# One transfer in place of eight for the negated row maxima of an attention step

## The chip, the cores and the metric

The kernel runs on one core of one Trainium2 chip. The metric is the device time of one execution in microseconds (us); the median of three runs of the kernel before is 1428.19 us (1427.73 to 1429.76). The engines are called as in the profile: PE is TensorE (matmuls), PEld its weight loads, DVE is VectorE, ACT is ScalarE, POOL is GpSimd, SP is SyncE, which here issues all DMAs.

## The reference

Two layers over x of shape (8, 512, 512), both conditioned on an embedding. Layer 0 is a linear attention (softmax of q over the features of a head, of k over the tokens). Layer 1 is the one that the change touches: 16 heads of 32, full attention over 512 tokens, with the softmax over the keys.

```
q = (xn @ q_w + q_b).reshape(Bx, Tx, H, -1)
k = (xn @ k_w + k_b).reshape(Bx, Tx, H, -1)
att = jnp.einsum('bnhl,bmhl->bnmh', q, k)
att = att + (1.0 - mask) * -1000000.0
att = jax.nn.softmax(att, axis=2)
v = ((xn @ v_w + v_b) * src_mask[:, :, None]).reshape(Bx, Tx, H, -1)
y = jnp.einsum('bnmh,bmhl->bnhl', att, v).reshape(Bx, Tx, Dx)
h = layer_norm(y, sb_norm_w, sb_norm_b) * (1.0 + scale) + shift
h = jax.nn.silu(h) @ out_w + out_b
return x + h
```

Everything is float32; products are made as three matmuls of high and low parts.

## The kernel before, in words

Layer 0 takes about the first 530 us. Layer 1 is cut into 32 steps: step n = 4b + g is the group g of four heads (j = 0..3) of batch b. Each step needs these items:

- `qk`: the q and k projections of the step, 12 matmuls each (lines 527 to 529), split into high and low parts by ACT (line 885) and DVE (line 1162, `sg_q`, `sg_k`), written to `stack_scratch` (lines 1491, 1492) and read back in stacked form into `Qs[n % 2]` and `Ks[n % 2]` (item `stack`, line 1504, 768 KB each).
- `S`: 16 matmuls (line 686) give the scores with queries on the partitions. DVE takes the negated maximum of each row from PSUM (line 1171, tile `cT`, which `nx` is a view of). ACT takes exp with this as bias (line 894) for the sum of the row only.
- `nxt`: the 16 columns of negated maxima (4 heads x 4 query tiles) are split into a high and a low part by three small DVE reductions (lines 1183, 1185, 1188, tile `nxs`), turned by a DVE transpose (line 1192, `nxT`), and written by SP into rows 98 and 99 of `Qs` (line 1524).
- `a`: 16 matmuls (line 694) give the transposed scores, keys on the partitions. They contract over 100 rows, and rows 98 and 99 subtract the maximum. ACT takes exp into `Pb` (line 904).
- `pv`: 128 small matmuls (line 712) of the step before, `tl` the transpose of their result (line 1199).

So the first `a` matmul of a step cannot start before the maxima of all 16 `S` tiles of that step are in `Qs`. This is called the handoff below. In the transpose before, the column t * 32 + s of `nxs` belongs to query tile t, and DVE turns blocks of 32x32; the maxima of 32 queries are then in four partitions of one block, and each of the two parts of each of four blocks goes by a DMA of its own, 16 pieces of 128 bytes. The eight DMAs of a step are issued back to back by SP.

Between the steps' own items lie the other products of layer 1: `v` (values of the next batch), `o` (output projection of the batch before), `tx` and `ty` (transposes, line 522). The order of all items is made by `the_order`: `weave` merges tracks of items by positions that the table `PLAN` gives, one entry for each g of 0 to 3, and names with a leading z for the last batch. Every engine works off its part of this one order, in order. PSUM has eight banks; the eighth is kept for `pv` in layer 1, seven are given in turn to the rest by `the_banks`, so a matmul may also wait for the reader of the bank's last content.

The wait at the handoff stands in `a` (on `nxq0` or `nxq1`), with a count of 128 for each use of a buffer. On SP the order is also strict: a DMA that stands behind the eight issues starts after them, among them the `stack` loads.

Of the kernel before, what the change touches and what calls it, by code (L numbers as in the profile page):

```python
# [20 lines left out]
RM, RX, RE = 96, 98, 100  # L21
# [20 lines left out]


PLAN = {
    "0k": ((0.157, 0.58), (0.489, 0.551)),
    "0v": ((0.811, 1.12), (0.011, 0.573)),
    "0q": ((0.678, 1.186), (0.109, 0.533), (1.018, 1.051)),
    "0o": ((0.808, 1.15), (0.725, 0.935), (0.176, 0.444)),
    "att": ((0.053, 0.062, 0.082, 0.233, 0.461), (0.01, 0.088, 0.245, 0.401, 0.741), (0.093, 0.109, 0.262, 0.692, 0.887), (0.349, 0.494, 0.559, 0.616, 0.645)),
    "pv": ((0.043,), (0,), (0,), (0.041,)),  # L50
    "tl": (None, (0.467, 1.131), (0.214, 0.217), (0.603, 0.7)),
    "tlx": ((0.277, 0.483), None, None, None),
    "ty": ((0, 0.854, 1.112), (0, 0.98, 1.049), (0, 1.11, 1.155), (0, 1.13, 1.169), (1, 0.038, 0.177)),
    "S": ((0.422, 0.55, 0.742, 0.811, 0.898), (0.396, 0.525, 0.936, 1.048, 1.099), (0.477, 0.9, 1.006, 1.108, 1.192), (0.066, 0.069, 0.727, 0.814, 0.999)),
    "nxt": ((0.923, 1.15), (1.106, 1.131), (1.173, 1.2), (1.183, 1.186)),
    "q": ((0.103, 0.141, 0.49), (0, 0, 0.086), (0.018, 0.115, 0.135), (0.049, 0.185, 0.238)),
    "k": ((0.527, 0.575, 0.782), (0.051, 0.192, 0.44), (0.243, 0.573, 0.583), (0.163, 0.432, 0.506)),
    "stack": ((1.2, 1.2), (0.696, 0.806), (0.756, 0.999), (0.602, 0.932)),
# [8 lines left out]
    "zatt": ((0.389, 0.877, 1.078, 1.121, 1.2), (0.088, 0.154, 0.355, 0.428, 0.525), (0.127, 0.319, 0.671, 1.024, 1.029), (0.181, 0.534, 0.601, 1.155, 1.2)),  # L67
    "zpv": ((0.273,), (0.111,), (0,), (0,)),
    "ztl": (None, (0.056, 1.025), (0.855, 1.141), (0.296, 0.516)),
    "ztlx": ((0.31, 0.95), None, None, None),  # L70
    "zty": ((0, 1.189, 1.2), (0, 1.199, 1.2), (1, 0, 0.319), (2, 1.157, 1.168), (3, 0.116, 0.835)),
    "zS": ((0.106, 0.211, 0.313, 0.395, 0.658), (0.55, 0.609, 0.778, 0.878, 1.016), (0.06, 0.243, 0.412, 0.43, 0.472), (0.163, 0.184, 0.449, 0.715, 0.933)),
    "znxt": ((1.063, 1.119), (1.183, 1.183), (1.14, 1.174), (0.381, 0.999)),
    "zq": ((0.487, 0.551, 0.824), (0.092, 0.2, 0.294), (0.518, 0.638, 1.2), (0.016, 0.077, 0.568)),
    "zk": ((0.834, 1.067, 1.139), (0.422, 0.431, 0.432), (0.295, 0.422, 0.904), (0.258, 0.961, 1.163)),
    "zstack": ((1.164, 1.192), (0.768, 1.042), (0.787, 1.2), (0.878, 1.019)),
    "tle": (None, None, None, (0.468, 0.924)),
    "zz": ((0.485, 0.776), (0.556, 0.808), (1.128, 1.2), (1.131, 1.2)),
    "lr": ((0.321, 0.774), None, None, None),
    "1v": ((0.569, 0.995), (0.143, 0.675), (0.449, 0.607)),  # L80
}


# [204 lines left out]
def cond_two_layers(nc, A, out):  # L288
# [4 lines left out]
    with ctx:  # L293
        def sb(name, shape, dt=F32, c=ctx):
            return c.enter_context(nc.sbuf_tensor(name, shape, dt))
# [38 lines left out]

        dn = sb("dn", [128, 2, NT, H1])
        nx = cT[:].rearrange("p a b -> p (a b)").rearrange("p (n j t s) -> p n j t s", n=2, j=4, s=2)
        nxs = sb("nxs", [128, NT, 32], FR)
        nxT = sb("nxT", [128, NT * 32])
        identr = sb("identr", [128, 128], FR)
        ident = identr[:].bitcast(F32)  # L340

# [31 lines left out]
        Qs, Ks = [None, None], [None, None]  # L373
# [139 lines left out]
        def _(e):  # L513
            def take(key):
                p = bank_before[key]
                if p is not None:
                    e.wait_ge(*done(p))
                return ps[bank_of[key]]
# [170 lines left out]
            def a(i, n, m, j):  # L689
                par = n % 2  # L690
                bank = take(("a", n, m, j))
                if m == 0 and j == 0:
                    e.wait_ge(s[f"nxq{par}"], 128 * (n // 2 + 1))
                e.matmul(bank[:], Ks[par][0:RE, j, m * 128:(m + 1) * 128], Qs[par][0:RE, j, :],  # L694
                         start=True, stop=True).then_inc(s["ST"], 1)

# [216 lines left out]
        def _(e):  # L913
# [317 lines left out]
            def tlx(i, b):  # L1231
# [7 lines left out]
                if i in (1, 3):  # L1239
# [112 lines left out]
        def _(e):  # L1352
# [232 lines left out]
```

## Time and profile before

| | before |
|---|---|
| median of 3 runs | 1428.19 us |
| profiled execution, its own time | 1433.99 us |
| span in the profile | 1432.2 us |
| mean granted TensorE clock | 0.955 of full |
| PE busy | 1322.4 us, 92% |
| DVE busy | 1023.1 us, 71% |
| ACT busy | 1001.6 us, 70% |
| POOL busy | 344.9 us, 24% |

Busy times are over the whole span. In layer 0 ACT does little, so its share in layer 1 is higher than 70%; the table by stretches in the rows below shows this. Idle time of an engine is named by what ended it. A chain of waits goes back from the last instruction to what released it at each step. In the table by stretches the five busy times are those of PE, PEld, DVE, ACT and POOL, in this order, and the granted clock (PEclk) is a share of full speed. The time between the span and the execution's own time, 1.8 us, lies around the kernel's instructions.

### The profile page before, as it was taken

The numbers are of one execution on the slowest core, as the hardware profiler recorded it, in microseconds if no ns is written. First come the engines' busy times: TensorE is split into PE (matmuls) and PEld (weight loads), VectorE is DVE, ScalarE is ACT, GpSimd is POOL, SyncE is SP. The second block draws the span as 40 slices with busy tenths as digits, with TensorE's granted clock in tenths as the row PEclk, the third lists the DMA queues.
The fourth block names the chain that finished last, engine by engine and source line by source line (L and its number), as shares of the span: only waits on it lengthen the run. The fifth ranks groups of instructions, "written<-read, shape, count | busy, mean of one in ns | idle before, by whom it ended". The sixth has DMA issues, their size and how long they took to land.

```text
span 1432.2 us, 25785 instructions
## 1 busy us (share of the span) xinstructions
PE 1322.4 (92%) x9592; PEld 1060.3 (74%) x9592; DVE 1023.1 (71%) x2025; ACT 1001.6 (70%) x2259; POOL 344.9 (24%) x367
## 2 busy tenths in 40 slices
PE   8899999999999988898998998998998898998898
PEld 5788888888888766576776776776776686676556
DVE  5887878888789874576766766756765865766555
ACT  4445445445455557897897887887897897898874
POOL 0323344234432520102402402402400500500203
PEclk9999999999999997998998998999999999999969
DMA  9011131111322455743544544544544454454412
GB/s 333 30 38 59 38 96 37 60 59 38 96 73 83 136 149 179 210 140 126 156 142 148 142 153 140 154 134 148 155 121 149 147 150 149 134 164 118 141 39 89
DMA packets 88029, 173.79 MB, mean 121 GB/s; under 512 B 12360, under 2 KB 12360, under 8 KB 87904
## 3 DMA queue, kind: packets, MB, share of 16 engines
q1 hardware_dynamic: 87904, 172.14, 39.3%
q8 instruction: 76, 1.25, 0.4%
q14 instruction: 49, 0.40, 0.1%
HBM read 104.45 MB, written 67.14 MB: 120 GB/s over the span
## 4 chain that ended last, share of the span: by engine, by line
PE 58%; DVE 17%; SPq 10%; DMA 7%; ACT 3%; issue 3%; POOL 1%; DVEq 0%; ACTq 0%; POOLq 0%
PE ps L527 12%; PE ps L529 12%; PE ps L528 12%; PE ps L694 9%; DVE cT L1171 8%; SPq L1524 8%; PE ps L686 5%; PE ps L522 3%; DMA Ks<-stack_scratch 3%; DMA Qs<-nxT 2%; PE ps L712 2%; ACT ps L894 1%; PE ps L636 1%; PE ps L615 1%; DMA mask_scratch<-vhl 1%
## 5 line engine op out<-in xcount | busy, mean ns | idle before, releaser
L1171 DVE TENSOR_REDUCE cT<-ps 128x1 f32<-128x512 f32 x512 | 323.3, 681 | 146.8 <-PE ps L686 146.0
L894 ACT ACTIVATE ps<-ps,cT 128x512 f32<-128x512 f32 x512 | 342.7, 683 | 35.8 <-DVE cT L1171 34.9
L904 ACT ACTIVATE Pb<-ps 128x512 f32<-128x512 f32 x512 | 269.1, 626 | 106.5 <-PE ps L694 103.6
L694 PE MATMUL ps<-Qs,Ks 100*128 100x512 f32 x512 | 182.3, 444 | 60.1 <-DMA Qs<-nxT 54.3
L686 PE MATMUL ps<-Ks,Qs 98*128 98x512 f32 x512 | 186.8, 428 | 21.9 <-ACT ps L894 10.1
L694 PEld LDWEIGHTS ps<-Qs,Ks 100*128 100x128 f32 x512 | 105.0, 210 | 101.7 <-issue 60.9
L686 PEld LDWEIGHTS ps<-Ks,Qs 98*128 98x128 f32 x512 | 98.3, 193 | 70.2 <-ACT ps L894 33.4
L1342 POOL TENSOR_TENSOR yb<-yb,cU 128x512 f32<-128x512 f32 x14 | 20.1, 1452 | 483.5 <-DVE cU L1215 483.5
L894 ACT ACTIVATION_READ_ACCUMULATOR ps<-ps,cT 128x1 f32 x512 | 116.1, 227 | 0.0
L527 PE MATMUL ps<-xTh,Wh_k 128*128 128x512 f32 x256 | 108.1, 422 | 6.8 <-DVE xTl L1022 3.7
L1266 POOL TENSOR_TENSOR rs<-ve,mhalf 128x4 f32<-128x4 f32 x32 | 32.6, 1019 | 334.0 <-DVE ve L990 218.0
L527 PE MATMUL ps<-Wh_o,sTh 128*128 128x512 f32 x256 | 103.6, 404 | 2.6 <-DVE sTl L1148 2.5
L527 PE MATMUL ps<-Wh_v,xTh 128*128 128x512 f32 x256 | 103.0, 402 | 0.0
L529 PE MATMUL ps<-xTh,Wl_k 128*128 128x512 f32 x256 | 102.1, 399 | 0.0
L528 PE MATMUL ps<-xTl,Wh_k 128*128 128x512 f32 x256 | 102.0, 399 | 0.0
L528 PE MATMUL ps<-Wl_o,sTh 128*128 128x512 f32 x256 | 100.7, 393 | 0.0
L528 PE MATMUL ps<-Wl_v,xTh 128*128 128x512 f32 x256 | 100.5, 393 | 0.0
L529 PE MATMUL ps<-Wh_v,xTl 128*128 128x512 f32 x256 | 100.5, 393 | 0.0
L529 PE MATMUL ps<-Wh_o,sTl 128*128 128x512 f32 x256 | 100.5, 393 | 0.0
L1308 POOL TENSOR_TENSOR wr<-wr,boB 128x512 f32<-128x512 f32 x64 | 82.9, 1313 | 9.8 <-DMA wr<-x_scratch 5.2
L1162 DVE SCALAR_TENSOR_TENSOR sg_q<-ps,cols,sg_q 128x512 fp32r<-128x512 f32 x32 | 23.9, 748 | 58.2 <-ACT sg_q L885 58.2
L1022 DVE TENSOR_TENSOR xTl<-ps,xTh 128x512 fp32r<-128x512 f32 x64 | 43.5, 689 | 29.8 <-ACT ps L774 29.7
(169 smaller groups left out, 2946.3 us busy)
## 6 DMA issues: line engine op xcount, KB each, us to landing
Qs<-stack_scratch SPq DMA_DIRECT2D x32, 768.0 KB
Ks<-stack_scratch SPq DMA_DIRECT2D x32, 768.0 KB
stack_scratch<-sg_q SPq DMA_DIRECT2D x32, 512.0 KB, 2.7
stack_scratch<-sg_k SPq DMA_DIRECT2D x32, 512.0 KB, 2.6
wr<-in_x SPq DMA_DIRECT2D x32, 256.0 KB, 4.9
x_scratch<-wr SPq DMA_DIRECT2D x32, 256.0 KB, 2.5
stack_scratch<-sg_q SPq DMA_DIRECT2D x32, 256.0 KB, 2.9
stack_scratch<-sg_k SPq DMA_DIRECT2D x32, 256.0 KB, 2.9
```

Of the source, the lines that this page charges most:

```text
L522: r = e.transpose(bank[:, t * 128:(t + 1) * 128], src, ident)
L527: e.matmul(bank[:], lh(k), rh(k), start=(k == 0), stop=False)
L528: e.matmul(bank[:], lh(k), rl(k), start=False, stop=False)
L529: return e.matmul(bank[:], ll(k), rh(k), start=False, stop=(k == NC - 1))
L686: e.matmul(bank[:], Qs[par][0:RX, j, t * 128:(t + 1) * 128], Ks[par][0:RX, j, :], start=True, stop=True).then_inc(s["S"], 1)
L694: e.matmul(bank[:], Ks[par][0:RE, j, m * 128:(m + 1) * 128], Qs[par][0:RE, j, :], start=True, stop=True).then_inc(s["ST"], 1)
L894: e.activation(bank[:], bank[:], ACT.Exp, bias=nx[:, n % 2, j, t, 0:1], accum_out=dn[:, b % 2, t, 4 * g + j:4 * g + j + 1]).then_inc(s["S_ ...
L904: e.activation(Pb[m][:, j, :], ps[bank_of["a", n, m, j]][:], ACT.Exp).then_inc(s["P"], 1)
L1022: e.tensor_tensor(xTl[:, c, :], ps[bank_of["tx", x, c]][:], xTh[:, c, :].bitcast(F32), ALU.subtract).then_inc(s["xT_lo"], 1)
L1171: e.tensor_reduce(nx[:, n % 2, j, t, 0:1], ps[bank_of["S", n, j, t]][:], AX.X, ALU.max, negate=True).then_inc(s["S_max"], 1)
L1308: e.tensor_tensor(wr[t][:], wr[t][:], boB[:], ALU.add).then_inc(s["xb"], 1)
L1524: e.dma_start(row.bitcast(F32), src).then_inc(s[f"nxq{par}"], 16)
```

## The change

Four things change in the code. The tile `nxs` becomes 32 columns wide (16 high, 16 low parts), column order head, query tile. The one transpose of 128x128 becomes four of 32x32, one for each group of 32 partitions, put side by side into `nxT` of 32 rows and 128 columns. One DMA moves these 32 rows of 512 bytes into rows 98 and 99 of `Qs`. The semaphore's count goes from 128 to 16 for each use. And the table `PLAN` has new numbers throughout.

```diff
-        nxs = sb("nxs", [128, NT, 32], FR)
-        nxT = sb("nxT", [128, NT * 32])
+        nxs = sb("nxs", [128, 32], FR)
+        nxT = sb("nxT", [32, 128])
...
                 if m == 0 and j == 0:
-                    e.wait_ge(s[f"nxq{par}"], 128 * (n // 2 + 1))
+                    e.wait_ge(s[f"nxq{par}"], 16 * (n // 2 + 1))
...
-                    m = nx[:, n % 2].rearrange("p j t s -> p t j s")
-                    hi = nxs[:, :, 0:4]
+                    m = nx[:, n % 2].rearrange("p j t s -> p (j t) s")
+                    hi, lo = nxs[:, 0:16], nxs[:, 16:32]
...
-                    e.transpose(nxT[:], nxs[:].rearrange("p t c -> p (t c)").bitcast(F32)).then_inc(s["nx_tr"], 1)
+                    for u in range(4):
+                        r = e.transpose(nxT[:, 32 * u:32 * u + 32], nxs[32 * u:32 * u + 32, :].bitcast(F32))
+                    r.then_inc(s["nx_tr"], 1)
...
-                    for u in range(4):
-                        for r in range(2):
-                            row = Qs[par][RX + r:RX + r + 1, :, :].rearrange("p j (t n) -> p j t n", t=NT)[:, :, :, 32 * u:32 * u + 32]
-                            src = nxT[32 * u + 4 * r:32 * u + 4 * r + 4, :].rearrange("j (t n) -> j t n", t=NT)
-                            e.dma_start(row.bitcast(F32), src).then_inc(s[f"nxq{par}"], 16)
+                    e.dma_start(Qs[par][RX:RE, :, :].bitcast(F32).rearrange("s j (t n) -> s (j t) n", t=NT),
+                                nxT[:]).then_inc(s[f"nxq{par}"], 16)
...
 PLAN = {
-    "nxt": ((0.923, 1.15), (1.106, 1.131), (1.173, 1.2), (1.183, 1.186)),
+    "nxt": ((0.889, 1.004), (1.116, 1.173), (1.195, 1.195), (1.074, 1.163)),
...
```

What stands on DVE ahead of the handoff to step 16 (the first step of a batch), before. `cT` are the row maxima, `bvB` the bias of the values (item `v`), `nxs` and `nxT` the parts of the maxima and their transpose; ps0 to ps7 are the banks.

```order
L1171 TENSOR_REDUCE cT<-ps4 128x1 [waits s_S]
L1171 TENSOR_REDUCE cT<-ps3 128x1 [waits s_S]
L1171 TENSOR_REDUCE cT<-ps2 128x1 [waits s_S]
L1070 TENSOR_TENSOR ps6<-ps6,bvB 128x512 [waits s_v_mm]
L1070 TENSOR_TENSOR ps1<-ps1,bvB 128x512 [waits s_v_mm]
L1183 TENSOR_REDUCE nxs<-cT 128x4x4 [waits s_S_max,s_nx_tr]
L1185 TENSOR_REDUCE cT<-nxs 128x4x4 [waits s_nx_hi]
L1188 TENSOR_REDUCE nxs<-cT 128x4x4 [waits s_nx_neg]
L1192 STREAM_TRANSPOSE nxT<-nxs 128x128 [waits s_nx_lo,s_nxq1]
```

And the same place on DVE now:

```order
L1171 TENSOR_REDUCE cT<-ps5 128x1 [waits s_S]
L1070 TENSOR_TENSOR ps0<-ps0,bvB 128x512 [waits s_v_mm]
L1171 TENSOR_REDUCE cT<-ps1 128x1 [waits s_S]
L1171 TENSOR_REDUCE cT<-ps6 128x1 [waits s_S]
L1183 TENSOR_REDUCE nxs<-cT 128x16 [waits s_S_max,s_nx_tr]
L1185 TENSOR_REDUCE cT<-nxs 128x16 [waits s_nx_hi]
L1188 TENSOR_REDUCE nxs<-cT 128x16 [waits s_nx_neg]
L1193 STREAM_TRANSPOSE nxT<-nxs 32x32 [waits s_nx_lo,s_nxq1]
L1193 STREAM_TRANSPOSE nxT<-nxs 32x32 x3
L1070 TENSOR_TENSOR ps4<-ps4,bvB 128x512 [waits s_v_mm]
```

The two additions of the values' bias stood between the last maximum and the splitting; now one stands ahead of the last two maxima and the other behind the transposes.

What SP issues around the handoff to step 17 (the second step of a batch), before. `sg_q` and `sg_k` are the projections on their way out, `Qs<-stack_scratch` and `Ks<-stack_scratch` the loads for the step after.

```order
L1491 DMA stack_scratch<-sg_q 128x1024 [waits s_q1_lo,s_stack0]
L1492 DMA stack_scratch<-sg_q 128x512
L1491 DMA stack_scratch<-sg_k 128x1024 [waits s_k1_lo,s_stack0]
L1492 DMA stack_scratch<-sg_k 128x512
L1524 DMA Qs1<-nxT 1x16x32 [waits s_nx_tr,s_ST]
L1524 DMA Qs1<-nxT 1x16x32 x7
L1504 DMA Qs0<-stack_scratch 96x4x512 [waits s_stq0,s_ST]
L1504 DMA Ks0<-stack_scratch 96x4x512 [waits s_stk0]
```

And now, at the same place on SP:

```order
L1493 DMA stack_scratch<-sg_q 128x1024 [waits s_q1_lo,s_stack0]
L1494 DMA stack_scratch<-sg_q 128x512
L1493 DMA stack_scratch<-sg_k 128x1024 [waits s_k1_lo,s_stack0]
L1494 DMA stack_scratch<-sg_k 128x512
L1522 DMA Qs1<-nxT 2x16x128 [waits s_nx_tr,s_ST]
L1506 DMA Qs0<-stack_scratch 96x4x512 [waits s_stq0,s_ST]
L1506 DMA Ks0<-stack_scratch 96x4x512 [waits s_stk0]
```

Nothing changed places here; the loads stand behind one issue in place of eight.

On PE the work between the last `S` matmul of a step and its first `a` matmul is nearly as before: three parts of `v` and `pv` at g = 0, three of `ty`, `pv` and three of `qk` at g = 1, `tx`, `pv` and two or three others at g = 2; at g = 3 four parts of `qk` and five `S` of the next step in place of six and six. In the first steps of the last batch there is more of it than before.

## Rows read from the trace of the kernel before

**Rows 1.** Table by stretches: us, then busy us (and count), PEclk, DMA share, GB/s.
```profile
0.00:530.00 530.00, 515.24 (x2752) 430.74 (x2753) 437.45 (x945) 266.27 (x528) 186.42 (x205) 0.99 0.28 89
...
860.00:970.00 110.00, 99.44 (x865) 79.55 (x864) 74.53 (x136) 93.15 (x221) 21.58 (x22) 0.95 0.49 145
```

**Rows 2.** The chain that ended last, by line, from the page.
```profile
PE ps L527 12%; PE ps L529 12%; PE ps L528 12%; PE ps L694 9%; DVE cT L1171 8%; SPq L1524 8%; PE ps L686 5%; PE ps L522 3%; DMA Ks<-stack_scratch 3%; DMA Qs<-nxT 2%; PE ps L712 2%; ACT ps L894 1%; PE ps L636 1%; PE ps L615 1%; DMA mask_scratch<-vhl 1%
```

**Rows 3.** Waits over the span: us in total, times, longest.
```profile
ACT Pb L904 <- PE ps L694: 103.6, 51, 7.9
...
PE ps L694 <- DMA Qs<-nxT: 54.3, 23, 5.0
...
PEld ps L686 <- ACT ps L894: 33.4, 70, 1.3
...
PE ps L686 <- DMA Ks<-stack_scratch: 8.4, 5, 2.1
```

**Rows 4.** Timeline, handoff to step 16: start, us, what [idle before <- releaser].
```profile
974.80 2.47 DVE L1171 TENSOR_REDUCE cT<-ps 128x1 f32<-128x512 f32 x4
...
978.08 3.70 PE L712 MATMUL ps<-Pb,vf 128*32 128x128 f32 x128
978.19 0.70 DVE L1070 TENSOR_TENSOR ps<-ps,bvB 128x512 f32<-128x512 f32 x1 [0.30 <-PE ps L529]
...
978.79 0.17 DVE L1183 TENSOR_REDUCE nxs<-cT 128x16 fp32r<-128x16 f32 x1
...
979.90 5.32 SPq L1524 DMA_DIRECT2D Qs<-nxT  x8
...
986.42 4.18 PE L694 MATMUL ps<-Qs,Ks 100*128 100x512 f32 x9 [4.64 <-DMA Qs<-nxT]
...
987.28 4.51 ACT L904 ACTIVATE Pb<-ps 128x512 f32<-128x512 f32 x9 [7.52 <-PE ps L694]
```

**Rows 5.** Timeline of PE: other handoffs, to steps 0, 18 and the last one.
```profile
536.93 4.18 PE L694 MATMUL ps<-Qs,Ks 100*128 100x512 f32 x9 [4.92 <-DMA Qs<-nxT]
...
1046.91 0.93 PE L694 MATMUL ps<-Qs,Ks 100*128 100x512 f32 x3 [1.18 <-DMA Qs<-nxT]
...
1373.73 0.47 PE L694 MATMUL ps<-Qs,Ks 100*128 100x512 f32 x1 [3.17 <-DMA Qs<-nxT]
```

**Rows 6.** Timeline of SP and PE at step 17, and the loads behind the issues.
```profile
1014.79 0.48 SPq L1504 DMA_DIRECT2D Ks<-stack_scratch  x1
...
1015.46 0.70 PE L694 MATMUL ps<-Qs,Ks 100*128 100x512 f32 x2
...
1023.98 0.77 PE L686 MATMUL ps<-Ks,Qs 98*128 98x512 f32 x1 [2.03 <-DMA Ks<-stack_scratch]
```

**Rows 7.** SP's issue times of line 1524, ns min/median/max.
```profile
L1524 SPq DMA_DIRECT2D Qs<-nxT x256: 623/623/768, 530.3 to 1390.3; - x128
```

**Rows 8.** Timeline of SP ahead of the handoff to step 19.
```profile
1058.20 0.32 SPq L1504 DMA_DIRECT2D Qs<-stack_scratch  x1
...
1068.44 5.32 SPq L1524 DMA_DIRECT2D Qs<-nxT  x8
```

**Rows 9.** Small DVE groups by shape: busy us, mean ns, idle before.
```profile
L1192 DVE STREAM_TRANSPOSE nxT<-nxs 128x128 f32<-128x128 f32 x32 | 10.0, 311 | 3.7 <-DVE nxs L1188 0.5
...
L965 DVE TENSOR_SCALAR mod<-ps,cols 128x8 f32<-128x8 f32 x8 | 1.2, 218 | 0.4 <-PE ps L550 0.4
...
L1044 DVE DVE_READ_ACCUMULATOR2_ANT kmx<- 128x1 f32 x32 | 2.6, 83 | 0.0
```

**Rows 10.** Table by stretches behind the handoff to step 16, columns as in Rows 1.
```profile
987.00:990.00 3.00, 3.00 (x9) 2.35 (x8) 2.37 (x7) 2.72 (x6) 0.00 (x0) 0.50 0.89 329
990.00:994.00 4.00, 4.00 (x13) 3.17 (x12) 0.00 (x0) 2.39 (x5) 0.00 (x0) 0.61 0.71 264
```

**Rows 11.** Timeline of ACT in the same stretch.
```profile
992.34 0.60 ACT L904 ACTIVATE Pb<-ps 128x512 f32<-128x512 f32 x1 [0.55 <-PE ps L694]
...
994.41 3.05 ACT L904 ACTIVATE Pb<-ps 128x512 f32<-128x512 f32 x6 [1.47 <-PE ps L694]
```

More of the change, by code:

```diff
@@ L44 @@
 PLAN = {
[L45 to L52, printed above, removed]
@@ L53 @@
-    "ty": ((0, 0.854, 1.112), (0, 0.98, 1.049), (0, 1.11, 1.155), (0, 1.13, 1.169), (1, 0.038, 0.177)),
-    "S": ((0.422, 0.55, 0.742, 0.811, 0.898), (0.396, 0.525, 0.936, 1.048, 1.099), (0.477, 0.9, 1.006, 1.108, 1.192), (0.066, 0.069, 0.727, 0.814, 0.999)),
-    "nxt": ((0.923, 1.15), (1.106, 1.131), (1.173, 1.2), (1.183, 1.186)),
-    "q": ((0.103, 0.141, 0.49), (0, 0, 0.086), (0.018, 0.115, 0.135), (0.049, 0.185, 0.238)),
-    "k": ((0.527, 0.575, 0.782), (0.051, 0.192, 0.44), (0.243, 0.573, 0.583), (0.163, 0.432, 0.506)),
@@ L58 @@
-    "stack": ((1.2, 1.2), (0.696, 0.806), (0.756, 0.999), (0.602, 0.932)),
[8 rows of a table removed]
[L67 to L79, printed above, removed]
@@ L80 @@
-    "1v": ((0.569, 0.995), (0.143, 0.675), (0.449, 0.607)),
+    "0k": ((0.063, 0.764), (0.503, 1.092)),
+    "0v": ((0.889, 1.145), (0.111, 0.562)),
+    "0q": ((0.659, 1.176), (0, 0.263), (1.065, 1.134)),
+    "0o": ((1.083, 1.166), (0.409, 1.001), (0.43, 0.514)),
+    "att": ((0.067, 0.22, 0.238, 0.274, 0.346), (0.092, 0.203, 0.203, 0.28, 0.842), (0.057, 0.091, 0.523, 0.582, 0.776), (0.194, 0.516, 0.534, 0.578, 0.583)),
+    "pv": ((0.02,), (0.012,), (0,), (0.031,)),
+    "tl": (None, (0.227, 0.827), (0.359, 0.894), (0.218, 0.556)),
@@ new lines @@
+    "tlx": ((0.202, 0.373), None, None, None),
+    "ty": ((0, 0.844, 0.993), (0, 0.971, 0.974), (0, 0.995, 1.056), (0, 1.098, 1.131), (1, 0.102, 0.57)),
+    "S": ((0.385, 0.541, 0.753, 0.843, 0.878), (0.428, 0.527, 0.815, 1.009, 1.08), (0.629, 0.928, 1.047, 1.186, 1.196), (0.047, 0.057, 0.759, 0.789, 0.966)),
+    "nxt": ((0.889, 1.004), (1.116, 1.173), (1.195, 1.195), (1.074, 1.163)),
+    "q": ((0.221, 0.255, 0.708), (0.046, 0.08, 0.125), (0.012, 0.092, 0.131), (0.041, 0.152, 0.248)),
+    "k": ((0.447, 0.553, 0.802), (0.2, 0.239, 0.462), (0.271, 0.409, 0.548), (0.358, 0.415, 0.53)),
@@ new lines @@
+    "stack": ((1.121, 1.174), (0.614, 0.861), (0.792, 1.063), (1.018, 1.032)),
[8 rows of a table added]
+    "zatt": ((0.516, 1.051, 1.154, 1.164, 1.2), (0.081, 0.676, 0.704, 0.834, 0.883), (0.629, 0.705, 0.878, 1.065, 1.076), (0.188, 0.286, 0.473, 0.724, 0.85)),
+    "zpv": ((0.186,), (0,), (0.158,), (0.332,)),
+    "ztl": (None, (0.768, 1.2), (0.525, 0.906), (0.525, 1.2)),
+    "ztlx": ((0.196, 1.045), None, None, None),
+    "zty": ((0, 1.199, 1.199), (0, 1.2, 1.2), (1, 0, 0.163), (1, 0.098, 0.64), (2, 0.352, 1.039)),
@@ new lines @@
+    "zS": ((0, 0.053, 0.168, 0.53, 0.58), (0.792, 0.945, 0.96, 1.031, 1.148), (0.084, 0.109, 0.136, 0.157, 0.367), (0.077, 0.089, 0.375, 0.382, 0.67)),
+    "znxt": ((0.958, 1.04), (1.12, 1.146), (0.405, 0.595), (0.228, 0.936)),
+    "zq": ((0.448, 0.642, 0.987), (0, 0.011, 0.271), (0.096, 0.394, 1.085), (0.249, 0.701, 1.13)),
+    "zk": ((0.627, 0.725, 0.955), (0.287, 0.345, 0.475), (0.093, 1.119, 1.2), (0.843, 0.898, 0.97)),
+    "zstack": ((1.129, 1.2), (0.821, 0.825), (0.61, 0.701), (0.131, 0.723)),
@@ L81 @@
+    "tle": (None, None, None, (1.021, 1.191)),
+    "zz": ((0.637, 0.772), (0.717, 0.973), (0.875, 1.2), (1.088, 1.2)),
+    "lr": ((0.093, 0.131), None, None, None),
+    "1v": ((0.21, 0.861), (0.354, 0.971), (0.113, 0.944)),
 }
@@ L1182, in nxt @@
                     e.wait_ge(s["S_max"], 16 * n + 16)
-                    e.tensor_reduce(hi, m[:, :, :, 0:1], AX.X, ALU.max).then_inc(s["nx_hi"], 1)
+                    e.tensor_reduce(hi, m[:, :, 0:1], AX.X, ALU.max).then_inc(s["nx_hi"], 1)
                     e.wait_ge(s["nx_hi"], n + 1)
-                    e.tensor_reduce(m[:, :, :, 1], hi.bitcast(F32).unsqueeze(3), AX.X, ALU.max, negate=True).then_inc(s["nx_neg"], 1)
+                    e.tensor_reduce(m[:, :, 1], hi.bitcast(F32).unsqueeze(2), AX.X, ALU.max, negate=True).then_inc(s["nx_neg"], 1)
                     e.wait_ge(s["nx_neg"], n + 1)
                     with nc.allow_low_precision(reason="the sum of a number and its negated high part is exact"):
-                        e.tensor_reduce(nxs[:, :, 4:8], m, AX.X, ALU.add).then_inc(s["nx_lo"], 1)
+                        e.tensor_reduce(lo, m, AX.X, ALU.add).then_inc(s["nx_lo"], 1)
                     if n:
-                        e.wait_ge(s[f"nxq{(n - 1) % 2}"], 128 * ((n - 1) // 2 + 1))
+                        e.wait_ge(s[f"nxq{(n - 1) % 2}"], 16 * ((n - 1) // 2 + 1))
                     e.wait_ge(s["nx_lo"], n + 1)
-                    e.transpose(nxT[:], nxs[:].rearrange("p t c -> p (t c)").bitcast(F32)).then_inc(s["nx_tr"], 1)
+                    for u in range(4):
+                        r = e.transpose(nxT[:, 32 * u:32 * u + 32], nxs[32 * u:32 * u + 32, :].bitcast(F32))
+                    r.then_inc(s["nx_tr"], 1)
             def tl(i, n):
```

16 rows, old and new, of the table PLAN are left out of this document.

## The prediction

> **What bounds the kernel now.** The page's shares name PE as the busiest engine. The table by stretches [rows 1] says where it isn't busy: layer 0 (530 us) has PE at 97% (515.24 / 530) and a clock of 0.99, so nothing is to be had there, and the change touches nothing there but the order. In layer 1 a batch of four steps takes about 110 us; PE is busy 99.4 of them, idle 10.6, with a mean clock of 0.95. A mean of 0.95 between the levels 2.4 and 1.2 GHz means 10% of the time at the lower one, 11 us, of which half, 5.5 us, are lost. ACT is busy 93.2 of 110, DVE 74.5. So layer 1 is bound by PE with ACT close behind.
>
> The chain [rows 2] shows what breaks PE's work: 8% of it (115 us) is SP issuing the maxima's DMAs, 2% their flight. The chain would promise over 100 us, but it charges the issues even where PE had other work meanwhile. The list of waits is the better measure [rows 3]: PE waited 54.3 us in 23 handoffs, the longest 5.0. ACT waited 103.6 us for the `a` matmuls, because it has nothing between its last `S` and the first `a`.
>
> The timeline of one handoff [rows 4] gives the parts. The last maximum ends at 974.80 + 2.47 = 977.27. Two bias additions follow, the second late by 0.30, so the splitting starts at 978.79, and 1.5 us have gone. Reductions, transpose (0.31, rows 9) and gaps take the 1.11 until 979.90, the eight issues last to 985.22, and 1.2 us later, at 986.42, PE starts. It had been free since 978.08 + 3.70 = 981.78. Of this kind (g = 0, waits of 4.6 to 5.0, the first at 536.93 [rows 5]) there are seven. At g = 2 the wait is about 1.2, in the last batch up to 3.2 [rows 5]. At g = 1 none is shown: PE has its own work until 1015.46 [rows 6].
>
> **Issues, eight to one.** An issue takes 0.623 [rows 7], the row of eight 5.32 [rows 4]. One issue of the new shape isn't in the trace: from below a stack load's 0.32 [rows 8], from above the longest of this line, 0.77 [rows 7]. I take 0.62, since it goes between the same tiles. That is 4.7 us off each handoff (bounds 4.55 to 5.0).
>
> **Transposes, one to four.** One of 128x128 takes 0.311. The trace has none of 32x32. From below, the shortest DVE instruction is 0.083, so four would be 0.33; from above, four at 0.311 are 1.24. The nearest row is the run of small operations without waits between them, 0.218 each [rows 9]: 0.87, so +0.56 a handoff (bounds 0.0 to 0.9). On DVE alone that is 18 us over 32 steps; DVE is busy 74.5 of 110, and its waits on PE hide it. It counts only as a later handoff.
>
> **Flight.** 32 pieces of 512 bytes in place of 128 of 128 bytes, 16 KB both times. From issue end to PE it was 1.2 [rows 4]. I keep 1.2, bounds 0.8 to 3.
>
> Four pieces of 512 bytes carry what sixteen of 128 did, which speaks for less; what could speak against it is the spread over DMA engines. The Trainium skill, "DMA: Bandwidth & Descriptors", section "Why a DMA increments its semaphore by 16 and not by 1", says that a DMA runs on the largest number of engines up to 16 that divides the slowest dimension of both sides. By that rule the new one, with 2 rows as target, uses 2 engines where the old ones used up to 4. No row here shows the engines of one DMA. If it doubled the flight, the sum would stay as it is, since the slack worked out next is over 1 us.
>
> **Handoff at g = 0 after the change.** The order now has no bias addition between last maximum and splitting (shown above). From 977.27: splitting and gaps 0.80 (1.11 - 0.31), transposes 0.87, issue 0.62, flight 1.2: ready at 980.8, PE free at 981.78. Slack 1.0 us; the wait of 4.64 is gone. At the other handoffs the waits, 3.2 at most [rows 5], are smaller than 4.7 - 0.56 = 4.1 us. What is late next is PE's own work ahead of `a`. I leave 2 us of residue in all: 54.3 - 2 = **52 us**.
>
> **Stack loads.** At g = 1 they stand behind the eight issues: issued at 1014.79, landed for PE at 1023.98, PE idle 2.03 [rows 6]. They now go 4.1 us earlier against PE's work, and waits of at most 2.1 vanish: 8.4 [rows 3], I take **8 us**.
>
> **Clock.** After the wait of 4.64 the granted clock is 0.50 from 987 to 990 and 0.61 in the next 4 us [rows 10]. With the wait gone, this fall goes. PE loses half of some 6.8 us there, 3.4, but ACT needs 0.50 for each exp (4.51 / 9), so that part is covered. What ACT lost is what it waited then, 0.55 and 1.47 [rows 11]: 2 us, seven times less one, **13 us** (bounds 0 and 7 x 3.4 = 24).
>
> **Given back.** 52 + 8 + 13 = 73 us over some 7.8 batches is 9.4 each: 110 becomes 100.6, where ACT needs 93.2 (93%) and PE 99.4 less its clock loss of 2 to 3. Two engines at 93 to 96% that pass seven banks to and fro wait more for each other than now, where PE's weight loads of line 686 waited 33.4 for ACT [rows 3], over 4 a batch. I take 2 us a batch more: **-15 us** (bounds 0 and -38, five a batch). The rest of the new order (layer 0, where `o`, `ty` and DMAs swap neighbours) I price at 0, hidden by PE's dense row of matmuls, bounds -5 and +5.
>
> **Sum.** 73 - 15 = 58. The profiled execution took 1434.0 (span 1432.2 and 1.8 around it): 1376. The median of the runs is 5.8 below it, so 1428.2 - 58 = **1370 us**.
>
> **Rivals.** *ACT takes over.* For it: ACT is at 85% already, and in the `S` part it goes without a gap. Against it: of its 16.8 us of idle time a batch most lies at the handoffs, which is just what is shortened (7.52 at g = 0 would become 2.9). If it gives back five a batch: 73 - 38 = 35, 1393 us.
>
> *Everything comes through.* The clock's whole 24 in place of 13, nothing given back, and the new order, made for the shorter handoff, gives as much: 52 + 8 + 24 = 84, 1344 us. For it: the bias additions have been taken out of the way. Against it: PE's and ACT's floors are both 93 to 95 us a batch.
>
> *The single DMA lands late* (the case of slower). Place: the flight at each handoff, behind the 768 KB loads. Those take 9.1 us from issue to landing (1014.79 to 1023.98, rows 6). If the small DMA had to wait in such a queue, the handoff would take 0.62 + 9.1 + 0.56 = 10.3 in place of 6.5, 3.8 us more, at 16 of the 32 handoffs (g = 2 and 3, whose loads go out before them) +61, while the other half gains 45 at most: 1444 us. It decides from a flight of 1.2 + 4.1 = 5.3 us on. Against it: at g = 3 the loads go out 10.2 us ahead of the maxima (1058.20 and 1068.44, rows 8), longer than they take.
>
> *It does nothing*: PE's cover is what counts and the new order puts as much into the way; 1428. Against it stands the 4.64 of pure idle time.
>
> **How the numbers follow.** The forecast (1352 to 1386 as its own range) has 0.56, ACT takes over 0.20, everything 0.16, lands late 0.05, nothing 0.03. 0.2% is about what a measurement can tell from no change. All but the last two are faster: faster 0.92, same 0.03, slower 0.05. The range for 8 in 10 takes most of both neighbours: 1342 to 1402.
>
> **What would show it.** PE's wait for the maxima's DMA falls from 54.3 to under 5; line 694's wait on it at g = 0 is gone, and the clock behind it stays 1.0; SP shows one issue of about 0.62 a step; four transposes of about 0.22 stand in a row; the wait for `Ks<-stack_scratch` is under 2; ACT's share in a batch rises from 85% to over 91%, with more waits of lines 686 and 694 on ACT. Wrong would be: a flight over 2.2 us, which ends the slack at g = 0; transposes of 0.31 or more with DVE late in the `S` part; a batch still at 105 us or more, with ACT at 93.

## The result, and the profile after

| | before | after |
|---|---|---|
| median | 1428.97 us (1427.73 to 1431.15, 4 runs) | 1350.51 us (1350.09 to 1354.27, 4 runs) |
| profiled execution | 1433.99 us | 1350.56 us |
| span | 1432.2 us | 1348.8 us |
| mean granted clock | 0.955 | 0.973 |

The ratio is 0.9455, 95% interval 0.9434 to 0.9476: 78 us less. The forecast was 1370 with a range of 1342 to 1402, so the time lies inside, but the gain is 78 where 58 were forecast. The profiled execution of the kernel before took 5 us more than its median, so differences between two profiles come out a few us larger than those between medians.

The page of the kernel after: the busy shares, and the chain that ended last by engine and by line.

```profile
PE 1306.4 (97%) x9592; PEld 1044.4 (77%) x9592; DVE 1029.0 (76%) x2121; ACT 994.5 (74%) x2259; POOL 346.2 (26%) x367
...
PE 69%; ACT 12%; DVE 10%; issue 2%; SPq 2%; DMA 2%; POOL 2%; DVEq 0%; POOLq 0%; ACTq 0%
PE ps L527 14%; PE ps L529 13%; PE ps L528 13%; PE ps L712 9%; ACT ps L894 7%; PE ps L694 6%; PE ps L686 6%; PE ps L522 6%; ACT Pb L904 3%; DVE cT L1171 2%; DVE st L1005 1%; PE ps L636 1%; PE ps L615 1%; POOL yb L1344 1%; DMA mask_scratch<-vhl 1%
```

SP's issues of the maxima had 8% of the chain [rows 2]; in the list by line they are gone. The small matmuls of `pv` (line 712, from 2% to 9%) and ACT have taken their place: the chain now runs through the work that lay beside the issues.

The table by stretches after, columns as in [rows 1]: layer 0, and 100 us of layer 1.

```profile
0.00:530.00 530.00, 514.68 (x2764) 430.61 (x2765) 434.60 (x951) 266.65 (x530) 187.71 (x205) 1.00 0.27 90
...
840.00:940.00 100.00, 98.25 (x868) 78.58 (x867) 76.53 (x148) 93.34 (x223) 21.97 (x23) 0.98 0.54 160
```

Layer 0 is as it was. In layer 1 the same 865 or so matmuls of a batch now take 100 us in place of 110; ACT is busy 93% and PE 98%.

The waits after, us in total, times, longest, against [rows 3]:

```profile
PEld ps L686 <- ACT ps L894: 48.8, 97, 1.6
ACT Pb L904 <- PE ps L694: 33.3, 25, 5.5
...
PE ps L694 <- DMA Qs<-nxT: 0.2, 1, 0.2
```

The wait for the maxima's DMA went from 54.3 to 0.2, the one for the stack loads is no longer in the list, and ACT's wait for the `a` matmuls went from 103.6 to 33.3. PE's weight loads wait 15 us more for ACT.

The timeline of a handoff at g = 0 (to step 4), which answers to [rows 4]:

```profile
631.27 1.28 DVE L1171 TENSOR_REDUCE cT<-ps 128x1 f32<-128x512 f32 x2
...
632.66 0.17 DVE L1183 TENSOR_REDUCE nxs<-cT 128x16 fp32r<-128x16 f32 x1
...
633.10 3.70 PE L712 MATMUL ps<-Pb,xin 128*32 128x128 f32 x128
633.36 0.84 DVE L1193 STREAM_TRANSPOSE nxT<-nxs 32x32 f32<-32x32 f32 x4
...
634.28 0.65 SPq L1522 DMA_DIRECT2D Qs<-nxT  x1
...
636.73 1.43 PE L694 MATMUL ps<-Qs,Ks 100*128 100x512 f32 x5
637.33 3.05 ACT L904 ACTIVATE Pb<-ps 128x512 f32<-128x512 f32 x6 [1.67 <-PE ps L694]
```

From the last maximum (632.55) to the end of the issue (634.93) it takes 2.4 us; it took 7.9 before (977.27 to 985.22), of which 1.4 were the two bias additions that the new order puts elsewhere. PE comes from `pv` and starts without a wait; ACT waited 7.52 there and waits 1.67.

The two instructions that are new, the first by line, as in [rows 7], ns min/median/max; the second by group, as in [rows 9]:

```profile
L1522 SPq DMA_DIRECT2D Qs<-nxT x32: 611/620/764, 526.7 to 1304.3; - x32
```

```profile
L1193 DVE STREAM_TRANSPOSE nxT<-nxs 32x32 f32<-32x32 f32 x128 | 25.6, 200 | 4.6
```

One way to read where the 83.4 us between the two spans went: PE's idle time (span less busy) fell from 109.8 to 42.4, and its busy time from 1322.4 to 1306.4 with the same 9592 matmuls. The second part goes with the clock: span times (1 - mean clock) is 64 us before and 36 after. The two measures (16 and 28 us) need not agree, since the mean runs over idle time as well.

### The profile page after: what moved, and what is told of

The parts are those of the page before. It is cut to its first block, busy times and chain, and to the rows that moved or that the text cites. A ratio compares the mean times of both kernels' runs of the same rounds, so it can differ in the third digit from the quotient of the medians.

```text
span 1348.8 us, 25657 instructions
## 1 busy us (share of the span) xinstructions
PE 1306.4 (97%) x9592; PEld 1044.4 (77%) x9592; DVE 1029.0 (76%) x2121; ACT 994.5 (74%) x2259; POOL 346.2 (26%) x367
## 4 chain that ended last, share of the span: by engine, by line
PE 69%; ACT 12%; DVE 10%; issue 2%; SPq 2%; DMA 2%; POOL 2%; DVEq 0%; POOLq 0%; ACTq 0%
PE ps L527 14%; PE ps L529 13%; PE ps L528 13%; PE ps L712 9%; ACT ps L894 7%; PE ps L694 6%; PE ps L686 6%; PE ps L522 6%; ACT Pb L904 3%; DVE cT L1171 2%; DVE st L1005 1%; PE ps L636 1%; PE ps L615 1%; POOL yb L1344 1%; DMA mask_scratch<-vhl 1%
## 5 line engine op out<-in xcount | busy, mean ns | idle before, releaser
L894 ACT ACTIVATE ps<-ps,cT 128x512 f32<-128x512 f32 x512 | 352.5, 770 | 21.9 <-DVE cT L1171 21.8
L904 ACT ACTIVATE Pb<-ps 128x512 f32<-128x512 f32 x512 | 271.1, 668 | 34.0 <-PE ps L694 33.3
L686 PE MATMUL ps<-Ks,Qs 98*128 98x512 f32 x512 | 198.3, 450 | 16.3 <-ACT ps L894 14.6
L894 ACT ACTIVATION_READ_ACCUMULATOR ps<-ps,cT 128x1 f32 x512 | 162.2, 317 | 0.0
L694 PE MATMUL ps<-Qs,Ks 100*128 100x512 f32 x512 | 159.0, 407 | 3.2 <-DVE sg_q L1162 1.3
L694 PEld LDWEIGHTS ps<-Qs,Ks 100*128 100x128 f32 x512 | 95.9, 189 | 38.1 <-ACT Pb L904 11.0
L1323 POOL TENSOR_TENSOR sTl<-yb,sTh 128x512 fp32r<-128x512 f32 x28 | 36.3, 1296 | 124.5 <-ACT sTh L873 124.5
```

The source lines that it names most:

```text
L686: e.matmul(bank[:], Qs[par][0:RX, j, t * 128:(t + 1) * 128], Ks[par][0:RX, j, :], start=True, stop=True).then_inc(s["S"], 1)
L894: e.activation(bank[:], bank[:], ACT.Exp, bias=nx[:, n % 2, j, t, 0:1], accum_out=dn[:, b % 2, t, 4 * g + j:4 * g + j + 1]).then_inc(s["S_ ...
L904: e.activation(Pb[m][:, j, :], ps[bank_of["a", n, m, j]][:], ACT.Exp).then_inc(s["P"], 1)
```

## The experiments

All ratios are to the kernel before. To put two versions side by side I take the difference of their ratios times 1429 us.

**The handoff alone, the table alone.** The two halves of the change, each without the other.

```diff
 # e_handoff: the changed kernel
-PLAN = {...}   # new
+PLAN = {...}   # of the kernel before
 # e_plan: the kernel before
-PLAN = {...}   # of the kernel before
+PLAN = {...}   # new
```

> The new handoff (one DMA, four transposes) with the table of the order of the kernel before. Theory (the handoff's latency is what counts, the new table only trims it): most of the 78 us comes, 1365 to 1380 us. Rival (the new table is needed, since the old order puts bias additions and other work into the way): under half of it, 1395 us or more.

> The new table of the order with the old handoff (one transpose, eight DMAs). Theory: within 10 us of 1428, since eight issues still delay the handoff by 4.7 us. Rival (the table brings much by itself): 1405 us or less.

The handoff alone: 1346.47 us, ratio 0.9414 (0.9398 to 0.9430). The table alone: 1435.95 us, ratio 1.0042 (1.0025 to 1.0060). So the new DMA and transposes bring 84 us, more than the whole change, and the new table costs 6 us, with either handoff: (0.9455 - 0.9414) x 1429 = 5.9 and 0.0042 x 1429 = 6.0. For e_handoff the theory's direction held, but its range of 1365 to 1380 was too slow by 18.5 us or more. For e_plan the theory's range (within 10 us of 1428) holds. The waits of e_handoff:

```profile
PEld ps L686 <- ACT ps L894: 38.3, 83, 1.9
ACT Pb L904 <- PE ps L694: 36.2, 22, 3.9
...
PE ps L694 <- DMA Qs<-nxT: 7.6, 7, 1.3
```

and of e_plan:

```profile
PE ps L694 <- DMA Qs<-nxT: 56.3, 28, 3.8
PEld ps L686 <- ACT ps L894: 48.1, 93, 1.6
```

This sorts out the 15 us that PE's weight loads wait more for ACT in the kernel after. With the new handoff alone they go from 33.4 [rows 3] to 38.3; with the new table alone to 48.1. Most of them come from the table, not from engines that press on each other once the handoff is short.

The page of e_handoff (first row) and its table by stretches:

```profile
PE 1297.0 (96%) x9592; PEld 1043.1 (78%) x9592; DVE 1040.2 (77%) x2121; ACT 995.5 (74%) x2259; POOL 344.9 (26%) x367
...
1030.00:1130.00 100.00, 97.77 (x868) 78.65 (x867) 77.41 (x149) 93.16 (x223) 21.60 (x22) 0.98 0.54 161
```

Its span is 1344.8. In PE's time the 87.4 us to the kernel before are 46.7 of waiting for the maxima's DMA (54.3 to 7.6), 8.4 for the stack loads (none left), 25.4 of busy time (1322.4 to 1297.0, with the clock up from 0.955 to 0.976) and 6.9 of other idle time. This says where PE's time went, not yet what each cause is worth.

The seven waits that are left are those at g = 0, where in the old table two bias additions stand ahead of the splitting. The timeline of one in e_handoff:

```profile
631.67 0.70 DVE L1070 TENSOR_TENSOR ps<-ps,bvB 128x512 f32<-128x512 f32 x1 [0.29 <-PE ps L529]
...
633.89 0.64 SPq L1522 DMA_DIRECT2D Qs<-nxT  x1
...
636.25 2.32 PE L694 MATMUL ps<-Qs,Ks 100*128 100x512 f32 x9 [0.98 <-DMA Qs<-nxT]
```

Here PE waits for the landing, so the flight can be read: 636.25 less 634.53 is 1.7 us, against 1.2 for the old form. The nine matmuls take 2.32, at full clock; before they took 4.18 [rows 4].

**More issues again.** The one DMA cut into four, and into eight.

```diff
-                    e.dma_start(Qs[par][RX:RE, :, :].bitcast(F32).rearrange("s j (t n) -> s (j t) n", t=NT),
-                                nxT[:]).then_inc(s[f"nxq{par}"], 16)
+                    for c in range(4):                    # e_split8: 8, w = 4
+                        r, u = divmod(c, 2)               # e_split8: 4
+                        dst = Qs[par][RX + r:RX + r + 1, :, :].bitcast(F32).rearrange("s j (t n) -> s (j t) n", t=NT)
+                        w = 8
+                        e.dma_start(dst[:, w * u:w * u + w, :], nxT[16 * r + w * u:16 * r + w * u + w, :]).then_inc(s[f"nxq{par}"], 16)
```

(with the counts of the two waits on `nxq` times four or eight)

> The changed kernel with its one DMA cut into four of eight rows: three issues more, 2.0 us later at each handoff. Theory (slack of about 1 us at the handoffs): 1 us late at those of g = 0 and little elsewhere, 1355 to 1370 us. Rival (no slack, every handoff counts in full): 32 x 2.0 = 64 us more, 1414 us. Rival (PE's cover is long, slack of 2 us and more): 1351 to 1354.

> The changed kernel with its one DMA cut into eight of four rows: it differs from the old handoff under the new table (1436 us) only in the four transposes and the pieces of 512 bytes. Theory (the number of issues makes the whole difference, the transposes add 0.5 us a handoff): 1436 to 1452 us. Rival (the transposes' form or the larger pieces carry part of the gain): 1425 or less.

Four: 1367.59 us, ratio 0.9557 (0.9539 to 0.9575), inside the theory's range. Eight: 1437.19 us, ratio 1.0071 (1.0050 to 1.0091), inside it as well. With eight issues the time is back at that of e_plan (1.0042), though the transposes are the new ones and the pieces 512 bytes. The issues and the first `a` matmuls at the same handoff (to step 4) in e_plan, e_split8 and e_split4:

```profile
644.60 5.32 SPq L1524 DMA_DIRECT2D Qs<-nxT  x8
...
651.12 2.47 PE L694 MATMUL ps<-Qs,Ks 100*128 100x512 f32 x5 [3.49 <-DMA Qs<-nxT]
```

```profile
648.42 4.90 SPq L1526 DMA_DIRECT2D Qs<-nxT  x8
...
654.49 2.04 PE L694 MATMUL ps<-Qs,Ks 100*128 100x512 f32 x4 [3.59 <-DMA Qs<-nxT]
```

```profile
637.35 2.69 SPq L1526 DMA_DIRECT2D Qs<-nxT  x4
...
641.31 0.94 PE L694 MATMUL ps<-Qs,Ks 100*128 100x512 f32 x3 [1.41 <-DMA Qs<-nxT]
```

From the last maximum to the first `a` matmul it takes 7.75 us in e_plan (from 643.37) and 7.81 in e_split8 (from 646.68): two handoffs of nearly the same length take the same time within their intervals. But they are equally long because two differences cancel. The four transposes take 0.84 in place of 0.31, and the eight issues 4.90 in place of 5.32 (573 ns each against 623). So e_split8 shows that the length of the row of issues carries the gain; it doesn't show that the form of the transposes is free. The next experiment bears on that.

The cost is bent. The time from the end of the issues to PE is 1.72 us with one DMA (see above), 1.27 with four and 1.17 with eight. With four, the issues end 2.06 us later than in the kernel after (2.69 less 0.63), so the maxima land 2.06 - 0.45 = 1.6 us later, 51 us over 32 handoffs, and this costs 0.0102 x 1429 = 15 us. With eight they land another 2.1 us later, 67 us in all, and this costs 0.0514 x 1429 = 73 us, all of it and a little more: PE's waits for the stack loads, 0.9 us in e_split4, are 5.3 in e_split8. The waits of e_split4 and e_split8 for the maxima:

```profile
PE ps L694 <- DMA Qs<-nxT: 13.9, 13, 1.4
```

```profile
PE ps L694 <- DMA Qs<-nxT: 60.5, 26, 4.0
```

The slack is not the same at every handoff. In the batch of steps 4 to 7, e_split4 waits 1.41 at g = 0 (above), not at all at g = 1 and 2, and 0.60 at g = 3; e_split8 waits 3.59 at g = 0 (above), 0.72, 0.91 and 2.81. The last of e_split4, then the three of e_split8:

```profile
721.04 0.47 PE L694 MATMUL ps<-Qs,Ks 100*128 100x512 f32 x1 [0.60 <-DMA Qs<-nxT]
```

```profile
683.78 0.47 PE L694 MATMUL ps<-Qs,Ks 100*128 100x512 f32 x1 [0.72 <-DMA Qs<-nxT]
...
712.41 1.17 PE L694 MATMUL ps<-Qs,Ks 100*128 100x512 f32 x4 [0.91 <-DMA Qs<-nxT]
...
740.93 0.47 PE L694 MATMUL ps<-Qs,Ks 100*128 100x512 f32 x1 [2.81 <-DMA Qs<-nxT]
```

Taken from the 1.6 and 3.7 us by which the maxima land later, the kernel after has a slack of about 0.1 to 0.2 us at g = 0, 1 at g = 3 and 3 at g = 1 and 2. This is why the first microseconds are cheap and the next ones are not.

**More transposes.**

```diff
                     for u in range(4):
+                        e.transpose(nxD[:, 32 * u:32 * u + 32], nxs[32 * u:32 * u + 32, :].bitcast(F32))
+                    for u in range(4):
                         r = e.transpose(nxT[:, 32 * u:32 * u + 32], nxs[32 * u:32 * u + 32, :].bitcast(F32))
```

> The changed kernel with four more transposes of 32x32 into a tile that nobody reads, ahead of the four: 0.84 us more on DVE and in each handoff. Theory (slack about 1 us, DVE 76% busy): 1351 to 1356 us. Rival (each handoff pays in full): 32 x 0.84 = 27 us more, 1377.

1362.38 us, ratio 0.9536 (0.9505 to 0.9567): 0.0081 x 1429 = 12 us more, of the 27 us that they last. This missed the theory's 1351 to 1356, and is far from full price. It is more per microsecond than the three extra issues cost (12 of 27 against 15 of 51, counted by the landing). Of the 11 us between the two profiles, 4.4 are idle time of PE (42.4 to 46.8; its waits for the maxima grew from 0.2 to 5.5, all at g = 0) and 6.6 are busy time (1306.4 to 1313.0), with a clock of 0.969 in place of 0.973. Why the clock is lower is open. The extra transposes stand on DVE and in the handoff at once, and no run here separates the two. By the same measure the step from one transpose (0.31) to four (0.84) is not free: 0.53 us a handoff, at 12 us for 0.84, is some 8 us, an estimate.

**The clock alone.** Work for PE in the wait of the kernel before, in the first step of batches 0 to 6.

```diff
                 if m == 0 and j == 0:
+                    if n % NG == 0 and n < 28:
+                        for _ in range(16):
+                            e.matmul(bank[:], Wh["q"][:, 0, 0:128], Wh["q"][:, 0, :], start=True, stop=True)
                     e.wait_ge(s[f"nxq{par}"], 128 * (n // 2 + 1))
```

> The kernel before, with 16 matmuls whose result is not used put on PE ahead of the wait for the maxima in the first step of batches 0 to 6 (3.7 us of work in the 4.6 us of waiting). Theory (the fall of the clock behind the wait costs 2 us each, 13 in all): 1411 to 1420 us, and a granted clock of 1.0 behind these handoffs. Rival (ACT sets the pace there, the clock costs nothing): 1426 to 1430. Rival (the whole 3.4 us each count): 1404.

1423.22 us, ratio 0.9944 (0.9923 to 0.9966): 8 us less, 5 to 11. Matmuls that compute nothing make the kernel faster. Table by stretches behind such a handoff (which began at 762.23), and the timeline of the `a` matmuls and of ACT:

```profile
763.00:770.00 7.00, 7.00 (x30) 5.16 (x28) 2.45 (x7) 7.00 (x16) 0.00 (x0) 1.00 0.82 291
```

```profile
757.28 3.92 PE L695 MATMUL ps<-Wh_q 128*128 128x512 f32 x16
762.23 2.36 PE L697 MATMUL ps<-Qs,Ks 100*128 100x512 f32 x9 [1.03 <-DMA Qs<-nxT]
...
762.83 7.95 ACT L907 ACTIVATE Pb<-ps 128x512 f32<-128x512 f32 x16 [7.51 <-PE ps L697]
```

The clock stays at 1.0 where it was 0.50 to 0.61 [rows 10], and ACT goes through its 16 exps in 7.95 us without the two waits of [rows 11]. The median lies 3 us above the theory's range, and both rivals, no effect (1426 to 1430) and the whole 3.4 us each (1404), are out.

**Which engine bounds the kernel after.** Less work for PE, and less for ACT. e_twoqk leaves out the product of high weights and low activations in layer 1's q and k; e_noacc leaves out the row sums (a constant 300 divides instead).

```diff
 # e_twoqk
                 e.matmul(bank[:], lh(k), rh(k), start=(k == 0), stop=False)
-                e.matmul(bank[:], lh(k), rl(k), start=False, stop=False)
+                if three:
+                    e.matmul(bank[:], lh(k), rl(k), start=False, stop=False)
...
-                r = product(ps[bank_of["qk", n, which]], channel_major(name, g), i)
+                r = product(ps[bank_of["qk", n, which]], channel_major(name, g), i, False)
 # e_noacc
-                e.activation(bank[:], bank[:], ACT.Exp, bias=nx[:, n % 2, j, t, 0:1],
-                             accum_out=dn[:, b % 2, t, 4 * g + j:4 * g + j + 1]).then_inc(s["S_exp"], 1)
+                e.activation(bank[:], bank[:], ACT.Exp, bias=nx[:, n % 2, j, t, 0:1]).then_inc(s["S_exp"], 1)
...
+                e.memset(dn[:], 300.0)
```

> The changed kernel without the products of high weights and low activations in layer 1's q and k projections: 256 matmuls of 512 columns less on PE, 58 us of its work at 0.23. Theory (PE bounds layer 1 now, ACT just behind): half to three quarters come through, 1307 to 1322 us. Rival (ACT and the banks bound it): under a quarter, 1336 or more. Rival (PE alone): all of it, 1293.

> The changed kernel without the row sums of layer 1's first exp (a constant stands in their place): ACT needs less for each of the 512. Theory (PE bounds layer 1): under a third of ACT's saving comes through, 1335 to 1350 us. Rival (ACT bounds it): ACT goes from 0.66 to about 0.5 a tile, 512 x 0.16 = 82 us, of which more than half comes through, 1310 or less.

e_twoqk: 1337.87 us, ratio 0.9359 (0.9330 to 0.9387), 14 us for 58 us of PE's work, so the time is that of the rival "ACT and the banks". PE's busy time fell by 21 us only (1306.4 to 1285.0, still 96% of the span), with a clock of 0.965 in place of 0.973, which is 11 us more lost by the measure above. Part of the 58 us is thus given back by the clock, and a busy share of 96% says little on how much work PE has. e_noacc: 1334.09 us, ratio 0.9336 (0.9311 to 0.9361), 17 us. ACT's busy time fell less than reckoned:

```profile
PE 1291.9 (97%) x9592; PEld 1041.4 (78%) x9592; DVE 1029.0 (77%) x2122; ACT 953.9 (72%) x1747; POOL 345.9 (26%) x367
```

From 994.5 to 953.9, 41 us in place of 82, so 41% came through; the time lies below the theory's range and the share above its third. Neither engine bounds layer 1 alone: most of the relief for either is lost again. To what isn't shown. No run relieves DVE or adds a bank, and the clock takes its part. The handoff was different: in it both stood still, and shortening it brought 84 us, more than the 54 + 8 that PE had waited.

**Where the new table loses.** Mixtures of the two tables with the new handoff: e_mix has the new entries for layer 0 and the stretch between the layers ("0k", "0v", "0q", "0o", "1v", "1t"), the old ones elsewhere; e_mixv has the new "v" as well, e_mixz the new entries of the last batch as well.

```diff
 # to the table of the kernel before: e_mix
+    "0k", "0v", "0q", "0o", "1v", "1t": new
 # e_mixv
+    "v": new
 # e_mixz
+    "z...", "tle": new
```

> The changed kernel with the new entries of the table for layer 0 and the stretch between the layers only, and those of the kernel before for layer 1. Theory (the new entries win 2 us up to the first handoff, where it came at 525.2 against 527.5, and lose 7 us over the steps of layer 1): 1343 to 1346 us, the fastest so far. Rival (the loss isn't in layer 1's entries): 1349 to 1352.

> The mixed table (new for layer 0, old for layer 1) with the new positions of the values' products as well, which take the bias additions out of the handoff at g = 0. Theory (the residual wait of 1.0 us at seven handoffs goes): 1337 to 1342 us. Rival (it is the position of the values' products that loses in the new table): 1346 or more.

> The mixed table with the new entries for the last batch as well. Theory (the new table loses its time in the middle batches, and puts more ahead of the late handoffs of the last): 1341 to 1344 us. Rival (the last batch's entries lose): 1346 or more.

e_mix: 1344.20 us, ratio 0.9410 (0.9385 to 0.9436). e_mixv: 1350.87, ratio 0.9458 (0.9435 to 0.9481). e_mixz: 1349.35, ratio 0.9454 (0.9435 to 0.9473). e_mix lies in its theory's range. The medians of the last two are 5 to 7 us above e_mix, outside their theories' ranges and inside those of the rivals, and their intervals touch its own at the edge. e_mixv was meant to remove the seven waits at g = 0 and did not:

```profile
PE ps L694 <- DMA Qs<-nxT: 6.1, 6, 1.3
```

Its edit did not do what it was made for. DVE's timeline at the handoff to step 16 in e_mixv:

```profile
931.22 0.69 DVE L1070 TENSOR_TENSOR ps<-ps,bvB 128x512 f32<-128x512 f32 x1
931.82 1.31 DVE L1171 TENSOR_REDUCE cT<-ps 128x1 f32<-128x512 f32 x2
933.80 0.70 DVE L1070 TENSOR_TENSOR ps<-ps,bvB 128x512 f32<-128x512 f32 x1 [0.67 <-PE ps L529]
934.41 0.16 DVE L1183 TENSOR_REDUCE nxs<-cT 128x16 fp32r<-128x16 f32 x1
```

One bias addition now stands ahead of the last two maxima, but the other still stands between them and the splitting, and waits 0.67 us for PE. So what a handoff at g = 0 without both additions is worth under the old table remains untested, and e_mixv says only that these places, without the rest of the new table, leave the waits and cost time. Why an entry loses is open; the positions act on each other, since both changes together with the rest cost no more than either alone.

**A faster version.** From e_mix, the low part by one subtraction.

```diff
-                    e.tensor_reduce(m[:, :, 1], hi.bitcast(F32).unsqueeze(2), AX.X, ALU.max, negate=True).then_inc(s["nx_neg"], 1)
-                    e.wait_ge(s["nx_neg"], n + 1)
-                    with nc.allow_low_precision(reason="the sum of a number and its negated high part is exact"):
-                        e.tensor_reduce(lo, m, AX.X, ALU.add).then_inc(s["nx_lo"], 1)
+                    e.tensor_tensor(lo, m[:, :, 0], hi.bitcast(F32), ALU.subtract).then_inc(s["nx_lo"], 1)
```

> The mixed table, and the low part of the maxima made by one subtraction (maximum less its high part) in place of two reductions (negation, then sum): about 0.2 us off each handoff. Theory (0.2 us of 32 handoffs, worth a third to a half, as the extra transposes and the three extra issues were): 1340 to 1343 us, against 1344.2. Rival (slack hides it all): 1344 to 1345. Rival (full price): 1337.

1340.59 us, ratio 0.9380 (0.9354 to 0.9405), 10 to 11 us below the kernel after and the fastest of all. Its distance to e_mix, 0.003 x 1429 = 4 us, is inside the intervals of the two; it lies where the theory put it, but isn't shown for itself.

## Why the prediction was right, and where it was off

- **What bounds.** Right in that the handoff is where PE stands still. Wrong in what was expected of the rest: the two light kernels show that neither PE nor ACT bounds by itself.
- **Issues.** 0.62 was taken, 0.620 is the median. 4.7 us off each handoff, as reckoned, and e_split8 shows that with eight issues the gain is gone.
- **Transposes.** 0.87 was taken for four, they take 0.84. That DVE hides their length is not borne out: four more of them cost 12 us in e_tr8.
- **Flight.** 1.2 was kept; where PE waits for it, it is 1.7. So a handoff got shorter by 3.7 us (4.7 - 0.5 - 0.5), not by 4.1, and half of the slack at g = 0 was eaten. The pieces of 512 bytes are not the reason: the DMAs of e_split4 and e_split8 have them too, eight or four each, and land after 1.27 and 1.17. The Trainium skill's page ("DMA: Bandwidth & Descriptors", "Why a DMA increments its semaphore by 16 and not by 1") would have the new DMA on fewer engines, and the longer flight goes with this, but no row shows the engines, and no run separates their number from that of the pieces. The rival of the late single DMA had its threshold at 5.3 and is far off.
- **Handoff at g = 0.** Ready at 3.5 us behind the last maximum was forecast, with PE free 1.0 later. In the kernel after 2.4 to the end of the issue and 1.7 of flight make 4.1, and PE comes 4.2 behind the last maximum (636.73 less 632.55). The wait is gone, with nearly nothing to spare.
- **52 us of waiting for the maxima.** 54.1 in the kernel after; 46.7 with the handoff alone, as the old order leaves 1 us at seven places. **8 us of stack loads:** 8.4.
- **13 us of clock.** Alone, in e_warm, it is 8 (5 to 11), so too large. ACT's part was read rightly: its 16 exps take 7.95 us there and took 10.2 before (987.28 to 997.46), 2.2 less at each of seven handoffs, but only about half of this came through. With the handoff short, PE's busy time falls by 25.4 us in e_handoff (16 in the kernel after). That is no measure of what the clock is worth: the loss by the clock (span times what is missing in the mean) goes from 64 to 32 in e_handoff, but in e_warm it also goes to 35 in the profiled execution and to 41 to 48 in the other three, and the kernel is only 8 us faster. Of the 64, the seven falls at g = 0, at 3.4 each, are 24; the rest lies elsewhere, and the prediction did not count it.
- **15 us given back.** This is the term that was wrong, in its sign as well. It was reckoned that two engines at 93% would hold each other up more, at 2 us a batch, a figure that no row gave. The new handoff alone raises PE's wait for ACT at line 686 by 5 us (33.4 to 38.3), not 15, and PE's idle time other than the two waits on DMAs falls by 6.9. The give-back that the kernel after does show comes with the new table, priced at 0 +/- 5 and worth 6 us of loss. Beyond the waits of 55 us that the new handoff removes, 29 us more came through, where 13 - 15 = -2 were forecast; how these 29 divide between the clock and the rest is open.

The signs that were named came: PE's wait for the maxima 0.2 us, one issue of 0.62, four transposes of 0.84 in a row, no wait for the stack loads in the list, ACT busy 93%. That the forecast missed the total by 20 us only is in part luck: the handoff brought 84 where 58 were forecast, and the new table took 6 back, which makes 78.

Of the rivals, "everything comes through" (52 + 8 + 24 = 84) describes the handoff alone: 84 us, 1346.5. It had nothing given back, as measured, though its 24 for the clock isn't shown, and its reason in the new order was wrong: that order did not help.

## What to carry to other kernels

Look for the time in which the two busiest engines stand still together and read from a timeline what is serial in it. Shortening that brought here more than PE had waited (84 us for 62), while relieving PE or ACT by itself brought 14 us of 58 and 17 of 41. Eight small DMAs of one queue were a serial chain of eight issues here, 0.57 to 0.64 us each for 2, 4 or 16 KB, and what stands behind them in the queue waits as well. Before a shorter chain is priced, read the slack at each place where it ends: here, of four handoffs, one had 0.1 us, one 1 us and two some 3. When a change comes with a new order of the work, run each half alone: here the order was a loss hidden in a large gain.

## What had not been expected of the hardware

One DMA of 32 pieces of 512 bytes from 32 partitions to 2 rows took as long to issue as one of 16 pieces of 128 bytes (0.620 and 0.623 us), but landed 1.7 us after the issue in place of 1.2. One of 4 pieces of 512 bytes, as many bytes as the 16 of 128, took 0.573 to issue. ACT's exp with a row sum costs 0.08 us more than without (41 us over 512), though the reading of the accumulator has a mean length of 0.23 us in the kernel before and 0.32 after: most of it lies beside the next exp. And 16 matmuls without use, 3.9 us of PE's time in a wait, at seven handoffs, made a kernel of 1430 us faster by 8.
